# Interleaving the first attention step's transposed scores with the score groups of the second and third step

## The chip, the cores and the metric

One core of one Trainium2 chip. The metric is the device time of one launch in microseconds, the median of the runs; the kernel before took 898.83 us (three runs, 896.07 to 898.97).

## The reference

One layer of gated cross attention and a gated feed-forward part, in float32, for 8 sequences of 256 tokens, 512 wide; 32 query heads of 16 dimensions share 8 groups of keys and values. Cut to what matters here (the weights are plain matrices, `g_x` and `g_f` scalars):

```python
q = (layernorm(x) @ Wq.T)             # 32 heads of 16
k, v = ctx @ Wk.T, ctx @ Wv.T         # 8 groups of 16, each used by 4 heads
score = einsum('bhqd,bhkd->bhqk', q, k) / sqrt(16)
attn = softmax(score)
x = x + tanh(g_x) * ((attn @ v) @ Wfc.T + bfc)
h = layernorm(x)
x = x + tanh(g_f) * (shared_mlp(h) + routed_mlp(h) * sum_of_top2_weights)
```

## The kernel before

The tokens are worked through in 4 blocks of 512 (two sequences each); attention comes first for all blocks, then the feed-forward part. The attention of a block has 8 steps (`STEPS`), a step being one of two sequences and one of four chunks of 8 heads. Steps are counted through the launch: step 0 is the first of all, `n` its number.

A step has two passes over its scores. In the first, `sm_pair` (line 1325) computes scores with queries on partitions; a step has four such pairs, v = 0 to 3, and each pair is four matmuls of line 1336 that fill two PSUM banks. VectorE takes the maximum over keys from each bank (`maximum`, line 902), 8 of them a step, into `mcol`. TensorE transposes `mcol` (`mt_job`), ScalarE copies it negated to `mT` (`m_copy`, line 684), and SyncE puts it by DMA as one more row beside the queries (`put_max`, line 330, semaphore `m_rd`). In the second pass `st_pair` (line 1351) computes the transposed scores, keys on partitions, with the maximum already subtracted, into the two banks `STB` = bank 2 and 3; ScalarE exponentiates them into `probs` (line 757, 8 a step, two a pair). `pv_unit` (line 1361) multiplies with the values, and VectorE turns and divides the result (`o_turn` 1024, `inverse` 1028, `divide` 1034 and 1039).

`sm_bank` (line 210) says which bank a score group takes. Steps 0 and 1 use bank 0 to 3 in turn, so `st_pair` of step 0 must wait until the maxima of both are taken. All later steps take turns on banks 0, 1 and 5, beside the transposed scores in 2 and 3.

Each engine runs its own list in the order in which it is written. TensorE's: the maxima's scores of step 0, `mt_job(0, 0)`, the scores of step 1, then `body`, whose step s issues the scores of step s + 2 pair by pair with the transposed scores of step s. Between them stand the jobs that prepare the next block: `x_job` (line 1281) transposes a normalised tile `xn` into PSUM bank 6, where ScalarE (`x_high`, into `xnT_h`) and VectorE (`x_low`, line 877, into `xnT_l`) read it; the next `x_job` waits until `x_low` of the one before has run (semaphore `x_lo`). VectorE's list has the 8 maxima of step 0, the 8 of step 1, then `norm_rows(1)` (line 925), on which ScalarE's first normalised tile of the next block (`xn_tile(1, 0)`, line 621) waits, and then in `body` the maxima of step s + 2 with the other work of the step; there `x_low(1, 0)` stands behind the sixth maximum of step 2, and `x_low(1, 1)` behind the first of step 3. ScalarE's list has `xn_tile(1, 0)` behind the second exponential of step 0. GpSimd subtracts the context's high part (`cx_low`, line 442) beside them. None of the lists of VectorE, ScalarE, GpSimd and SyncE is touched.

Of the kernel before, what the change touches and what calls it, by code (L numbers as in the profile page):

```python
# [14 lines left out]
TILES = BLOCK // P  # L15
HC = P // DH
CHUNKS = HEADS // HC
# [3 lines left out]
UNITS = 8  # L21
# [22 lines left out]
def build(nc, x, ctxT, wq, wk, wv, wfc, bfc, g_x, g_f, w_gu, w_dn, w_r, out):  # L44
# [6 lines left out]
    with ExitStack() as ctx:  # L51
        def sem(name):
            return ctx.enter_context(nc.semaphore(name))
# [99 lines left out]
        bank = [ctx.enter_context(nc.psum_tensor(f"bank{i}", [P, 512], f32)) for i in range(8)]  # L153
# [17 lines left out]
        q_rd = [sem(f"q_rd{c}") for c in range(CHUNKS)]  # L171
        k_rd = [sem("k_rd0"), sem("k_rd1")]
        m_rd = sem("m_rd")
# [8 lines left out]
        xn_ok, x_tr, x_hi, x_lo, xb_ok = sem("xn_ok"), sem("x_tr"), sem("x_hi"), sem("x_lo"), sem("xb_ok")  # L182
        q_pr, q_hi, q_lo = sem("q_pr"), sem("q_hi"), sem("q_lo")
        k_pr, k_hi, k_lo = sem("k_pr"), sem("k_hi"), sem("k_lo")
        v_cp, vt_tr, vt_cp = sem("v_cp"), sem("vt_tr"), sem("vt_cp")
        f_mm, f_add, ln2_stats, ln2_var = sem("f_mm"), sem("f_add"), sem("ln2_stats"), sem("ln2_var")

        sm_full, st_full, max_ok = [sem("sm_full0"), sem("sm_full1")], [sem("st_full0"), sem("st_full1")], sem("max_ok")
        mt_tr, mt_cp = sem("mt_tr"), sem("mt_cp")
# [19 lines left out]

        def sm_bank(n, s, u):  # L210

            return bank[u % 4] if isinstance(n, int) and n < 2 else bank[(0, 1, 5)[(UNITS * s + u) % 3]]

        def x_bank(tb, j):

            return bank[j] if isinstance(tb, int) and tb == 0 else PJ[0]
# [656 lines left out]
        def _(dve):  # L873
# [22 lines left out]
            def maximum(n, s, u, par):  # L896
                qt, half, e = u // 4, u // 2 % 2, u % 2
                dve.wait_ge(sm_full[e], UNITS // 2 * n + u // 2 + 1)
                if u == 0 and not (isinstance(n, int) and n < 2):
                    dve.wait_ge(mt_tr, n - 1)  # L900
                at = mcol[:, par, e * HC + half * RH:e * HC + (half + 1) * RH].rearrange("p (j t) -> p j t", t=2)
                v.tensor_reduce(at[:, :, qt], sm_bank(n, s, u)[:, :].rearrange("p (r k) -> p r k", r=2),  # L902
                                AX.X, ALU.max).then_inc(max_ok, 1)
# [366 lines left out]
        def _(pe):  # L1270
# [9 lines left out]
            def tr(out, in_):  # L1280
                return nc.tensor.transpose(out, in_, ident[:, :])  # L1281

            def x_job(tb, j):
                pe.wait_ge(xn_ok, TILES * tb + j + 1)
                for c in range(DC):
                    last = tr(x_bank(tb, j)[:, c * P:(c + 1) * P], xn[:, j, c * P:(c + 1) * P])
                last.then_inc(x_tr, 1)
# [35 lines left out]
            def sm_pair(n, s, v, bb, c):  # L1323

                qt, half = v // 2, v % 2
                if isinstance(n, int) and n < 2:
                    if UNITS * n + 2 * v >= 4:
                        pe.wait_ge(max_ok, UNITS * n + 2 * v - 2)  # L1330
                else:
                    pe.wait_ge(max_ok, UNITS * n + 2 * v - (0 if s == 0 and v == 0 else 1))
                for j in range(2):
                    for e in range(2):
                        rows = slice(e * ROWS, e * ROWS + SM)
                        last = mm(sm_bank(n, s, 2 * v + e)[:, j * S:(j + 1) * S],  # L1336
                                  q_st[rows, c, 2 * half + j, qt * P:(qt + 1) * P], k_st[rows, bb, c, :],
                                  start=True, stop=True)
                        if j == 1:
                            last.then_inc(sm_full[e], 1)  # L1340

            def st_pair(n, v, bb, c):

                kt, half = v // 2, v % 2
                if isinstance(n, int) and n == 0 and v == 0:
                    pe.wait_ge(max_ok, 2 * UNITS)
                else:
                    pe.wait_ge(exp_ok, UNITS * n + 2 * v)
                for e in range(2):
                    rows = slice(e * ROWS, e * ROWS + ST)  # L1350
                    mm(STB[e][:, :], k_st[rows, bb, c, kt * P:(kt + 1) * P], q_st[rows, c, 2 * half:2 * half + 2, :],  # L1351
                       start=True, stop=True).then_inc(st_full[e], 1)

            def pv_unit(n, p, bb, c):

                kt, g2 = p // 2, p % 2
                pe.wait_ge(exp_ok, UNITS * n + 4 * kt + 4)
                if p == 0 and not (isinstance(n, int) and n == 0):
                    pe.wait_ge(ob_ok, n)
                for r in range(RH):  # L1360
                    last = mm(OTB[32 * r:32 * r + VW, g2 * S:(g2 + 1) * S], vals[:, bb, kt, 2 * c + g2, :],  # L1361
                              probs[:, p, r, :], start=p == 0, stop=kt == 1, skip_group_check=True)
                last.then_inc(pv_ok, 1)

            def mt_job(n, par):

                pe.wait_ge(max_ok, UNITS * n + UNITS)
                if not (isinstance(n, int) and n < 2):
                    pe.wait_ge(ob_ok, n - 1)
                tr(OTB[0:16, 0:P], mcol[:, par, :]).then_inc(mt_tr, 1)  # L1370
# [46 lines left out]
            for v in range(UNITS // 2):  # L1417
                sm_pair(0, 0, v, 0, 0)
            pe.wait_ge(q_lo, 3)
            mt_job(0, 0)  # L1420
            pe.wait_ge(q_rd[1], 64)
            for v in range(UNITS // 2):
                sm_pair(1, 1, v, 0, 1)
            pe.wait_ge(q_lo, CHUNKS)

            def body(t, first, last):
                nx = t + 1
                for s in range(STEPS):
                    n = STEPS * t + s
# [2 lines left out]
                    te = t if e < STEPS else nx  # L1432
                    be, ce = e % STEPS // CHUNKS, e % CHUNKS
                    look = not last or e < STEPS
                    for v in range(UNITS // 2):
                        if look:
                            if v == 0:
                                pe.wait_ge(q_rd[ce], 64 * (2 * te + be + 1))
                                pe.wait_ge(k_rd[be], 64 * (te + 1))
                            sm_pair(n + 2, e % STEPS, v, be, ce)  # L1440
                        if v == 0:
                            pe.wait_ge(m_rd, 32 * (n + 1))
                        st_pair(n, v, bb, c)
                        if v == 0 and not (first and s == 0):
                            for p in (2, 3):
# [77 lines left out]
                            continue  # L1523

                        if s == 0 and v == 1:
                            if first:
                                pe.wait_ge(k_lo, 1)
                            else:
                                pe.wait_ge(f_add, TILES * t - 2)
                            x_job(nx, 0)  # L1530
                        if s == 0 and v == 3:
                            pe.wait_ge(x_lo, TILES * nx + 1)
# [46 lines left out]
                        if s == 7 and v == 3:  # L1579
# [3 lines left out]
                            vt_job(nx, 0)  # L1583

            blocks(pe, body)

            for qt in range(2):
# [208 lines left out]
```

## Time and profile before

| | |
|---|---|
| median of the three runs | 898.83 us (896.07 to 898.97) |
| the profiled execution: its own time | 898.2 us |
| its span | 895.9 us |
| mean granted TensorE clock | 0.986 of full |
| TensorE matmuls busy | 864.9 us, 97% |
| VectorE busy | 636.0 us, 71% |
| ScalarE busy | 337.6 us, 38% |
| GpSimd busy | 480.7 us, 54% |

The span runs from the first to the last instruction; 2.3 us of the execution's own time lie around it. Starts are in us from the beginning of the span. A busy share is a mean over the launch: the stretch that the change touches begins near 38 us, where step 0's maxima are done, and it has to be read by itself.

### The profile page before, as it was taken

The page shows a single profiled execution, that of the slowest core. Times are in us where ns is not written, and L with a number is a line of the kernel's source. Part 1 is how long each engine was busy: PE and PEld are TensorE (multiplying, and loading weights), DVE is VectorE, ACT ScalarE, POOL GpSimd, SP SyncE. Part 2 cuts the span into 40 slices and gives each one's busy share as a digit, 9 for nine tenths or more (in the row PEclk, how much of TensorE's full clock was granted, in tenths as well). Part 3 has the DMA queues.
Part 4 walks back from the last instruction along what each step waited for, and adds up shares of the span by engine and source line. Part 5 has one row for each costly group of instructions (what it writes and reads, how often), then busy time and mean ns, then how long its engine had stood idle before and what let it go on. Part 6 is the DMA issues. An engine that isn't in the chain of part 4 may idle for free.

```text
span 895.9 us, 14888 instructions
## 1 busy us (share of the span) xinstructions
PE 864.9 (97%) x4923; PEld 643.1 (72%) x4923; DVE 636.0 (71%) x1085; ACT 337.6 (38%) x636; POOL 480.7 (54%) x485
## 2 busy tenths in 40 slices
PE   8699999999999899999999999998999999999998
PEld 6445665665565457888888888885788888888886
DVE  7789899889889956656565656667656565656565
ACT  4186586677657842212111211344211221122111
POOL 2314003002104999778667866754966786678640
PEclk9779999999999999999999999999999999999999
DMA  7753332432422113111211121112221112111102
GB/s 277 241 164 103 123 116 61 155 124 78 136 87 70 37 48 95 45 50 47 70 39 55 47 66 45 54 48 86 79 67 45 53 47 64 42 58 47 47 1 94
DMA packets 43609, 71.88 MB, mean 80 GB/s; under 512 B 6064, under 2 KB 21936, under 8 KB 43312
## 3 DMA queue, kind: packets, MB, share of 16 engines
q1 hardware_dynamic: 43568, 71.34, 24.6%
q8 instruction: 24, 0.39, 0.2%
q14 instruction: 17, 0.14, 0.0%
HBM read 55.33 MB, written 15.73 MB: 79 GB/s over the span
## 4 chain that ended last, share of the span: by engine, by line
PE 82%; DVE 11%; issue 3%; ACT 2%; DMA 1%; SPq 1%; POOL 0%; DVEq 0%; ACTq 0%; POOLq 0%
PE bank L1276 24%; PE bank L1277 23%; PE bank L1278 23%; DVE mcol L902 5%; PE bank L1336 4%; PE bank L1361 4%; PE bank L1351 3%; PE bank L1281 1%; DVE oN L1034 1%; PE bank L1670 1%; ACT probs L757 1%; DVE oB L1024 1%; DVE x_l L1241 1%; DMA q_scr<-qx_l 1%; DVE xnT_l L877 0%
## 5 line engine op out<-in xcount | busy, mean ns | idle before, releaser
L1276 PE MATMUL bank<-x_l,w_h 128*128 128x512 f32 x504 | 197.5, 392 | 2.5 <-DVE u L1112 2.5
L1278 PE MATMUL bank<-x_h,w_h 128*128 128x512 f32 x504 | 196.4, 390 | 0.0
L1277 PE MATMUL bank<-x_h,w_l 128*128 128x512 f32 x504 | 196.4, 390 | 0.0
L902 DVE TENSOR_REDUCE mcol<-bank 128x2 f32<-128x512 f32 x256 | 164.5, 670 | 25.2 <-PE bank L1336 24.5
L616 ACT ACTIVATE hT_h<-bank 128x512 fp32r<-128x512 f32 x72 | 43.1, 599 | 361.1 <-DVE bank L1214 352.2
L757 ACT ACTIVATE probs<-bank 128x512 f32<-128x512 f32 x256 | 139.0, 596 | 74.4 <-PE bank L1351 72.6
L572 POOL TENSOR_TENSOR w_l<-raw,w_h 128x512 fp32r<-128x512 f32 (+1 forms) x144 | 162.0, 1157 | 2.9
L1124 DVE SCALAR_TENSOR_TENSOR xa<-bank,tgf,xa 128x512 f32<-128x512 f32 x128 | 96.1, 751 | 77.7 <-PE bank L1278 77.6
L1276 PE MATMUL bank<-dn_l,hT_h 128*128 128x512 f32 x288 | 112.1, 389 | 1.7 <-issue 1.7
L1276 PEld LDWEIGHTS bank<-x_l,w_h 128*128 128x128 f32 x504 | 94.6, 188 | 25.9 <-DVE u L1112 3.9
L1278 PE MATMUL bank<-dn_h,hT_h 128*128 128x512 f32 x288 | 112.0, 389 | 0.0
L1277 PE MATMUL bank<-dn_h,hT_l 128*128 128x512 f32 x288 | 112.0, 389 | 0.0
L1278 PEld LDWEIGHTS bank<-x_h,w_h 128*128 128x128 f32 x504 | 94.7, 188 | 19.9
L1277 PEld LDWEIGHTS bank<-x_h,w_l 128*128 128x128 f32 x504 | 94.8, 188 | 19.1
L1112 DVE TENSOR_TENSOR u<-bank,r 128x512 f32<-128x512 f32 x72 | 49.7, 690 | 69.2 <-PE bank L1278 69.2
L442 POOL TENSOR_TENSOR cx_l<-cx_raw,cx_h 128x512 fp32r<-128x512 f32 x12 | 15.4, 1283 | 150.4 <-ACT cx_h L616 150.4
L581 POOL CAST dn_h<-dnraw 128x512 fp32r<-128x512 f32 x36 | 22.1, 613 | 111.6 <-PE bank L1278 93.8
L1336 PEld LDWEIGHTS bank<-k_st,q_st 48*128 48x128 f32 x512 | 40.2, 194 | 58.1 <-DVE mcol L902 38.4
L569 POOL CAST w_h<-raw 128x1792 fp32r<-128x1792 f32 x36 | 63.6, 1768 | 29.7 <-DVE x_l L1241 17.9
L1336 PE MATMUL bank<-k_st,q_st 48*128 48x256 f32 x512 | 66.7, 341 | 12.8 <-DVE mcol L902 11.6
L1361 PE MATMUL bank<-probs,vals 128*32 128x256 f32 x1024 | 70.1, 392 | 0.0
L1112 DVE TENSOR_TENSOR c<-bank,u 128x512 f32<-128x512 f32 x72 | 49.4, 686 | 24.0 <-PE bank L1278 23.9
(144 smaller groups left out, 1343.8 us busy)
## 6 DMA issues: line engine op xcount, KB each, us to landing
raw<-w_gu SPq DMA_DIRECT2D x36, 512.0 KB, 3.3
dnraw<-w_dn SPq DMA_DIRECT2D x36, 256.0 KB, 2.6
q_st<-q_scr SPq DMA_DIRECT2D x64, 128.0 KB, 2.6
q_scr<-qx_h SPq DMA_DIRECT2D x16, 256.0 KB, 2.1
q_scr<-qx_l SPq DMA_DIRECT2D x16, 256.0 KB, 2.3
q_st<-q_scr SPq DMA_DIRECT2D x64, 64.0 KB, 2.7
out<-xa SPq DMA_DIRECT2D x16, 256.0 KB, 2.0
cx_raw<-ctxT SPq DMA_DIRECT2D x14, 256.0 KB, 2.9
```

The costliest lines, as they stand in the source:

```text
L569: g.tensor_copy(w_h[f][:, :, :], raw[f][:, 0:7, :]).then_inc(gu_hi, 1)
L572: last = g.tensor_tensor(w_l[f][:, part, :], raw[f][:, part, :], w_h[f][:, part, :].bitcast(f32), ALU.subtract)
L616: return nc.scalar.activation(out, in_, ACT.Copy)
L757: nc.scalar.activation(probs[:, p, 2 * half:2 * half + 2, :], STB[e][:, :].rearrange("p (r q) -> p r q", r=2), ACT.Exp, scale=float(DH) ** ...
L902: v.tensor_reduce(at[:, :, qt], sm_bank(n, s, u)[:, :].rearrange("p (r k) -> p r k", r=2), AX.X, ALU.max).then_inc(max_ok, 1)
L1112: return v.tensor_tensor(out, psum[:, :], part[:, :], ALU.add)
L1124: v.scalar_tensor_tensor(tile, source[:, :], scale, tile, ALU.mult, ALU.add).then_inc(acc_ok, 1)
L1276: mm(out, a_h, b_l, start=start, stop=False, skip_group_check=onto)
L1277: mm(out, a_l, b_h, start=False, stop=False, skip_group_check=onto)
L1278: return mm(out, a_h, b_h, start=False, stop=stop, skip_group_check=onto)
L1336: last = mm(sm_bank(n, s, 2 * v + e)[:, j * S:(j + 1) * S], q_st[rows, c, 2 * half + j, qt * P:(qt + 1) * P], k_st[rows, bb, c, :], start= ...
L1361: last = mm(OTB[32 * r:32 * r + VW, g2 * S:(g2 + 1) * S], vals[:, bb, kt, 2 * c + g2, :], probs[:, p, r, :], start=p == 0, stop=kt == 1, s ...
```

## The change

`sm_bank` gives banks 0, 1 and 5 to step 1 as well; only step 0 keeps banks 0 to 3. The first transposed scores of step 0 then wait for the maxima of step 0 only. The body's step 0 of the first block is written out in `first_step`: the last two score pairs of step 1, and the first two of step 2, each stand ahead of a pair of step 0's transposed scores, and the last two pairs of step 2 follow behind them, with `x_job(1, 1)` between the two. `x_job(1, 0)` and `mt_job(1, 1)` change places. The wait for `q_lo` at 4 stands ahead of step 1's scores, as bank 5 was the last home of a query product.

```diff
         def sm_bank(n, s, u):
 
-            return bank[u % 4] if isinstance(n, int) and n < 2 else bank[(0, 1, 5)[(UNITS * s + u) % 3]]
+            return bank[u % 4] if isinstance(n, int) and n == 0 else bank[(0, 1, 5)[(UNITS * s + u) % 3]]
...
                 qt, half = v // 2, v % 2
-                if isinstance(n, int) and n < 2:
-                    if UNITS * n + 2 * v >= 4:
-                        pe.wait_ge(max_ok, UNITS * n + 2 * v - 2)
+                if isinstance(n, int) and n == 0:
+                    if v >= 2:
+                        pe.wait_ge(max_ok, 2 * v - 2)
                 else:
                     pe.wait_ge(max_ok, UNITS * n + 2 * v - (0 if s == 0 and v == 0 else 1))
...
                 if isinstance(n, int) and n == 0 and v == 0:
-                    pe.wait_ge(max_ok, 2 * UNITS)
+                    pe.wait_ge(max_ok, UNITS)
                 else:
                     pe.wait_ge(exp_ok, UNITS * n + 2 * v)
...
             pe.wait_ge(q_rd[1], 64)
-            for v in range(UNITS // 2):
+            pe.wait_ge(q_lo, CHUNKS)
+            for v in range(2):
                 sm_pair(1, 1, v, 0, 1)
-            pe.wait_ge(q_lo, CHUNKS)
+
+            def first_step():
+
+                for v in range(UNITS // 2):
+                    if v < 2:
+                        sm_pair(1, 1, v + 2, 0, 1)
+                    else:
+                        if v == 2:
+                            pe.wait_ge(q_rd[2], 64)
+                        sm_pair(2, 2, v - 2, 0, 2)
+                    if v == 0:
+                        pe.wait_ge(m_rd, 32)
+                    st_pair(0, v, 0, 0)
+                    if v == 1:
+                        pe.wait_ge(k_lo, 1)
+                        x_job(1, 0)
+                        pe.wait_ge(mt_cp, 1)
+                        mt_job(1, 1)
+                    if v == 2:
+                        pe.wait_ge(vt_cp, 1)
+                        pe.wait_ge(mt_cp, 2)
+                        for p in (0, 1):
+                            pv_unit(0, p, 0, 0)
+                sm_pair(2, 2, 2, 0, 2)
+                pe.wait_ge(x_lo, TILES + 1)
+                x_job(1, 1)
+                sm_pair(2, 2, 3, 0, 2)
...
                     look = not last or e < STEPS
+                    if first and s == 0:
+                        first_step()
+                        continue
                     for v in range(UNITS // 2):
```

TensorE's list before, from the transpose of step 0's maxima (`mcol`) on. `bank<-k_st,q_st` are score groups (four to a pair), `bank<-q_st,k_st` transposed scores (two to a pair), `probs,vals` the product with the values, `xn` an `x_job`.

```order
L1281 MATMUL bank<-ident,mcol 16x128
L1336 MATMUL bank<-k_st,q_st 128x256 x20
L1351 MATMUL bank<-q_st,k_st 128x512 x2
L1336 MATMUL bank<-k_st,q_st 128x256 x4
L1351 MATMUL bank<-q_st,k_st 128x512 x2
L1281 MATMUL bank<-ident,mcol 16x128
L1281 MATMUL bank<-ident,xn 128x128 x4
L1336 MATMUL bank<-k_st,q_st 128x256 x4
L1351 MATMUL bank<-q_st,k_st 128x512 x2
L1361 MATMUL bank<-probs,vals 32x256 x8
```

The four pairs of step 1 and the first of step 2 stand together as 20 matmuls, ahead of the first transposed scores.

The same place after the change, up to the second `x_job`:

```order
L1281 MATMUL bank<-ident,mcol 16x128
L1336 MATMUL bank<-k_st,q_st 128x256 x12
L1351 MATMUL bank<-q_st,k_st 128x512 x2
L1336 MATMUL bank<-k_st,q_st 128x256 x4
L1351 MATMUL bank<-q_st,k_st 128x512 x2
L1281 MATMUL bank<-ident,xn 128x128 x4
L1281 MATMUL bank<-ident,mcol 16x128
L1336 MATMUL bank<-k_st,q_st 128x256 x4
L1351 MATMUL bank<-q_st,k_st 128x512 x2
L1361 MATMUL bank<-probs,vals 32x256 x8
```

Only three pairs (12 matmuls) stand ahead of the first transposed scores; `x_job` now stands ahead of the transpose of `mcol`.

The end of step 0 and the start of step 1, as the difference of the two lists:

```order
-L1336 MATMUL bank<-k_st,q_st 128x256 x4
-L1351 MATMUL bank<-q_st,k_st 128x512 x2
+L1336 MATMUL bank<-k_st,q_st 128x256 x4
 L1281 MATMUL bank<-ident,xn 128x128 x4
-L1336 MATMUL bank<-k_st,q_st 128x256 x4
+L1336 MATMUL bank<-k_st,q_st 128x256 x8
```

Before, all pairs of step 2 stood ahead of the second `x_job`; now its last pair stands behind it, together with the first pair of step 3.

## Rows read from the trace of the kernel before

**Rows 1.** The page: busy time in us, share of the span and instructions of the engines
```profile
PE 864.9 (97%) x4923; PEld 643.1 (72%) x4923; DVE 636.0 (71%) x1085; ACT 337.6 (38%) x636; POOL 480.7 (54%) x485
```

**Rows 2.** Chain that ended last, 30 to 90 us: start, us, what
```profile
39.32 4.29 DVE mcol L902 x7
...
56.81 1.12 ACT probs L757 x2
...
62.74 0.69 DVE mcol L902
...
81.59 0.61 DVE mcol L902
82.20 0.04 issue
82.25 0.51 PE bank L1336 x4
```

**Rows 3.** VectorE in order of time: start, us, engine, operation, [idle before, releaser]
```profile
39.32 4.87 DVE L902 TENSOR_REDUCE mcol<-bank 128x2 f32<-128x512 f32 x8 [1.28 <-PE bank L1336]
44.12 0.15 DVE L925 SCALAR_TENSOR_TENSOR nmr<-mv,rstd 128x8 f32<-128x8 f32 x1
...
49.00 1.29 DVE L902 TENSOR_REDUCE mcol<-bank 128x2 f32<-128x512 f32 x2 [1.60 <-PE bank L1336]
50.21 0.68 DVE L877 TENSOR_TENSOR xnT_l<-bank,xnT_h 128x512 fp32r<-128x512 f32 x1
...
53.35 0.69 DVE L902 TENSOR_REDUCE mcol<-bank 128x2 f32<-128x512 f32 x1
```

**Rows 4.** TensorE in order of time, 38 to 53 us
```profile
41.86 0.80 PE L1336 MATMUL bank<-k_st,q_st 48*128 48x256 f32 x4 [0.40 <-DVE mcol L902]
43.74 0.79 PE L1336 MATMUL bank<-k_st,q_st 48*128 48x256 f32 x4 [1.09 <-DVE mcol L902]
44.34 0.80 PE L1351 MATMUL bank<-q_st,k_st 49*128 49x512 f32 x2
...
47.01 0.38 PE L1281 MATMUL bank<-ident,mcol 128*16 128x128 f32 x1
47.18 1.06 PE L1281 MATMUL bank<-ident,xn 128*128 128x128 f32 x4
48.17 0.80 PE L1336 MATMUL bank<-k_st,q_st 48*128 48x256 f32 x4
48.76 0.63 PE L1351 MATMUL bank<-q_st,k_st 49*128 49x512 f32 x2
49.33 1.93 PE L1361 MATMUL bank<-probs,vals 128*32 128x256 f32 x16
51.19 0.78 PE L1336 MATMUL bank<-k_st,q_st 48*128 48x256 f32 x4
...
52.13 0.66 PE L1281 MATMUL bank<-ident,xn 128*128 128x128 f32 x4
52.84 0.51 PE L1336 MATMUL bank<-k_st,q_st 48*128 48x256 f32 x4
```

**Rows 5.** ScalarE in order of time, 45 to 47 us
```profile
45.14 1.08 ACT L757 ACTIVATE probs<-bank 128x512 f32<-128x512 f32 x2 [6.19 <-PE bank L1351]
46.11 0.81 ACT L621 ACTIVATE xn<-xa,nmr,rstd 128x512 f32<-128x512 f32 x1
```

**Rows 6.** SyncE's issue of the maxima's row; landing times of the `q_st` transfers, 30 to 60 us
```profile
38.97 1.49 SPq L330 DMA_DIRECT2D q_st<-mT  x2
...
DMA to landing us min/median/max: 2.5/3.1/5.4
```

**Rows 7.** Stretches: PE, PEld, DVE, ACT, POOL busy (instructions), granted clock, DMA share, GB/s
```profile
34.00:35.00 1.00, 0.25 (x4) 0.04 (x2) 1.00 (x3) 0.00 (x0) 1.00 (x2) 0.87 0.66 206
40.00:41.00 1.00, 0.34 (x2) 0.34 (x4) 1.00 (x3) 0.00 (x0) 0.00 (x0) 0.50 0.02 4
51.00:52.00 1.00, 1.00 (x10) 0.70 (x6) 0.00 (x0) 0.00 (x0) 0.00 (x0) 0.59 0.90 270
57.00:58.00 1.00, 0.21 (x6) 0.03 (x2) 1.00 (x2) 1.00 (x4) 0.97 (x1) 1.00 0.51 134
59.00:60.00 1.00, 1.00 (x12) 0.21 (x4) 1.00 (x3) 1.00 (x3) 0.00 (x0) 0.50 0.02 4
62.00:82.00 20.00, 18.38 (x164) 10.55 (x162) 19.79 (x36) 14.84 (x30) 2.90 (x3) 1.00 0.23 69
```

**Rows 8.** GpSimd and VectorE near 57 us; all of L1034, ns min/median/max
```profile
57.03 1.27 POOL L442 TENSOR_TENSOR cx_l<-cx_raw,cx_h 128x512 fp32r<-128x512 f32 x1 [19.03 <-ACT cx_h L616]
57.05 1.52 DVE L1034 TENSOR_TENSOR oN<-oB,rden 128x256 f32<-128x256 f32 x1
...
L1034 DVE TENSOR_TENSOR oN<-oB,rden x31: 400/408/1540, 57.1 to 327.0; 128x256 f32<-128x256 f32 x31
```

More of the change, by code:

```diff
@@ L1525, in body @@
                         if s == 0 and v == 1:
[L1526 to L1529, printed above, removed]
+                            pe.wait_ge(f_add, TILES * t - 2)
                             x_job(nx, 0)
```

## The prediction

> **What bounds the kernel now.** I read the page first, then the chain of waits, then each engine in order of time. The page says that TensorE's matmuls are busy 97% of the span and VectorE 71% [rows 1], so on the whole TensorE is the bound. The chain of the stretch from 30 to 90 us says otherwise for that stretch: it runs over the maxima on VectorE, over ScalarE near 57 us, over VectorE again from 62.74 us, and only at 82.25 us does TensorE take over [rows 2]. From 62 to 82 us VectorE is busy 19.79 of 20 us while TensorE has 1.62 us without a matmul [rows 7]. VectorE's list has no slack there, so **whatever VectorE loses before 62.74 us, TensorE gets 82.25 us later by the same amount, and behind that point TensorE is the bound**. The question is therefore at what time VectorE, which does its work in an unchanged order, reaches fixed marks of its list. I use two: the first maximum of step 3, at 53.35 us [rows 3], and the maximum at 62.74 us [rows 2].
>
> From within the microsecond 34 to within the microsecond 51, and again around 60, TensorE runs at the lower of its two clocks, 1.2 GHz: 34 and 51 show the passages (0.87 and 0.59 as means), and 59 shows 0.50 [rows 7]. Durations for the change's place come from rows at that level.
>
> **Costs that I use.** At the low clock a score pair at 48.17 lets VectorE start at 49.00, 0.83 us later, and its successor on TensorE start after 0.59 us [rows 3, 4]. At the full clock the pair at 52.84 lets VectorE start at 53.35, 0.51 us later. A pair of maxima takes 1.29 us, of which the first is 0.69 [rows 3]. Transposed scores lead to an exponential 0.80 us later, two of which take 1.08 us [rows 4, 5]. The product with the values holds TensorE 1.86 us (49.33 to 51.19), `x_job` 0.99 us (47.18 to 48.17), the transpose of the maxima 0.17 us [rows 4]. TensorE answers a maximum in about 0.06 us, my estimate from the successions in these rows.
>
> **Part 1: step 1's scores on three banks.** Before, two pairs are computed ahead of need and the 8 maxima run without a gap, 39.32 to 44.12 us [rows 3]. With banks 5, 0, 1 the second pair's second half needs bank 5 back, so it starts only after the first maximum, at 40.07; VectorE can go on at 40.88, not 40.61. The third pair starts at 41.63 (maximum at 42.44). Then the first transposed scores follow at 42.23, and the fourth pair waits for the fifth maximum, 43.13: it starts at 43.19, and VectorE ends the eight at 45.29. That is three gaps of about 0.27 to 0.3 us and a pair that is itself answered late: **the maxima of step 1 end 1.17 us later** than 44.12. The moved wait for `q_lo` costs nothing: the split it guards stands behind the second maximum of step 0 in VectorE's list, well ahead of 39.32 us.
>
> **Part 2: the exponentials start earlier, but stop at once.** The first two start at 43.03 instead of 45.14 [rows 5], 2.1 us earlier, and end at 44.11. ScalarE's next item is the tile `xn`, which waits for `norm_rows(1)`, and that stands behind the eighth maximum: 45.42 instead of 44.27. So the tile runs 45.45 to 46.25 instead of from 46.11 [rows 5]: the 2.1 us have shrunk to 0.7.
>
> **Part 3: step 2's maxima come late.** Before, its first pair stood with step 1's scores at 43.74, and by 50.29 VectorE had taken six of the eight [rows 3, 4]. Now `x_job` (46.31) and the transpose of the maxima (47.3) stand ahead of the first pair: it starts at 47.5, and VectorE, idle since 45.8, takes two maxima from 48.3 to 49.6. Transposed scores (48.1) and the product with the values (48.7 to 50.5) come next, then the second pair at 50.5, and VectorE takes maxima from 51.35 to 52.65. At 52.65 it has taken four, where before it had taken six, and split a tile, by 50.9. The third pair needs bank space from the maximum that ends at 52.04; at 52.1, at the full clock, it gives maxima 52.65 to 53.9.
>
> **Part 4: the second `x_job` is now a barrier in front of the last pair.** It waits for `x_low(1, 0)`, which VectorE has behind the sixth maximum: 53.9 to 54.5 (0.68 us [rows 3]; before it ran at 50.21). `x_job` starts at 54.6 and the last pair 0.7 us behind it (52.13 to 52.84 [rows 4]), at 55.3: maxima 55.8 to 57.1. The first pair of step 3 waits for the seventh of them, 56.5, and VectorE starts step 3 at 57.05 if the clock is full. If it is low, `x_job` takes 0.99 and each pair 0.83, and it starts at 57.97. Against 53.35 this is **3.7 to 4.6 us later**. TensorE has a matmul in only about 1.6 of the 4.65 us from 51.7 to 56.35; before, the clock fell in a microsecond with 0.25 busy and behind one with 0.21 [rows 7], so I expect it to fall here, somewhere inside, and take 4.1.
>
> The moved DMAs: SyncE's list is the same, its waits for `mt_cp` come within 0.4 us of before, and the reads for step 4 move with the product they wait for, by about the same 3 to 4 us as their users.
>
> **Part 5: what step 1 gives back.** At 57.05 `divide` took 1.52 us, while its median over 31 is 0.408: 1.11 us more, beside GpSimd's subtraction from 57.03 to 58.30 [rows 8]. GpSimd follows ScalarE, which moves by less than VectorE, so that the two overlap for part of that time only: I give back 0.7 of a possible 1.1 us. The Trainium skill, SBUF — State Buffer, section on who interferes with whom, says that a VectorE operation with two SBUF inputs and a GpSimd operation that reads SBUF exclude each other for the whole instruction, so the later one waits until the other ends; by it the return is 0 if `divide` comes just behind GpSimd's start and all of it if it comes behind its end, and the trace agrees with it: `divide` ends 0.27 us behind GpSimd's end. The waits for low-clock matmuls in step 1 stay in either kernel; the bounds on their difference are 0.25 us less (none left) and nothing.
>
> **Sum:** 4.1 − 0.7 = **3.4 us**, between 3.7 − 1.35 = 2.35 and 4.6. The profiled execution took 898.2 us, so the forecast is **901.6 us**. The median of the runs is 0.6 us above that execution; a difference of 0.3%, about what a measurement of this kernel can tell from no change, is 2.7 us.
>
> **The rivals.**
> *The early exponentials win (not slower).* The chain passes over ScalarE near 57 us [rows 2], and if ScalarE set the pace up to there, an earlier start would count. For it: the last exponentials of step 0 start by my times at 51.9 instead of 52.24. Against it: VectorE has 19.79 of 20 us filled behind it, and has more left to do at 52 us. If VectorE's lag is taken up before 62.74, what stays is ScalarE's 0.3 us: 897.9 us; with the whole contention of `divide` gone too, 1.1 us more, 896.8. It decides if step 3's maxima start by 53.4.
> *The clock comes back one stage earlier.* TensorE works without a gap from 46.3 instead of 47.0 us. Full clock from 48 us on would halve the product with the values to 1.0 and shorten each answer by 0.3: step 3's maxima then start near 55.8, 2.4 late, less 0.4 given back: 900.2 us.
> *The clock doesn't come back at 51.4.* The third pair then takes 0.83, `x_job` 0.99: 1.3 us more than the mean case, 903 us with what is given back.
> *The first transposed scores don't come earlier at all.* They wait for `m_rd`. Its transfers are issued 38.97 to 40.46 us and need 2.5 to 5.4 us by the other `q_st` transfers [rows 6]: from the second issue, 39.7, that is 42.2 to 45.1. At 42.2 nothing is lost. At 45.1 the fourth pair, queued behind them on TensorE, would start at 45.7 instead of 43.19, and everything behind it 2.5 us later: 904.1 us. The DMA engines were busy 0.02 of the microsecond 40 [rows 7], so I take the short end. The Trainium skill, DMA: Bandwidth & Descriptors, in the anatomy of one DMA, has a fixed cost of about 2 us, most of it the receipt of the write; by it the row lies there at 41.7 or, from the end of the issue, 42.5, and this rival is nearly excluded.
>
> **How the numbers follow.** My forecast's case has 0.65: of its span, 2.35 to 4.6, three quarters lie over 2.7 us, so 0.49 slower and 0.16 no difference. ScalarE's rival 0.11: its own times are no difference, 0.06; the other 0.05 stand for more than it gives, under 895.5 us.  The early clock 0.10, same. The late clock 0.09 and the late row 0.05, both slower. Together: 0.05 faster, 0.32 same, 0.63 slower. The range of 8 in 10 reaches from 898.6, which takes in the early clock and leaves out most of ScalarE's rival, to 903.9, just short of the late row.
>
> **What would show each step right or wrong.** Right: the eighth maximum of step 1 ends near 45.3 us; the first exponential starts near 43.0 and the tile near 45.5; VectorE stands idle over 2 us ahead of step 2's first maximum at 48.3, and over 1 us ahead of its seventh, put down to TensorE's scores; step 3's first maximum starts at 57 to 58; TensorE takes over the chain at 85 to 87 us, and from there on the two traces run in parallel. Wrong: if step 3's maxima start near 53 us; or if they start at 57 and the end is still the same, because time is found between 62 and 82 us that the rows show as filled; or if the first transposed scores wait for a DMA until 45 us.

## The result, and the profile after

| | before | after |
|---|---|---|
| median (5 runs each) | 898.83 us | 901.86 us |
| lowest to highest | 896.07 to 899.24 | 901.17 to 903.22 |
| profiled execution: own time, span | 898.2, 895.9 us | 901.17, 899.3 us |
| mean granted clock | 0.986 | 0.987 |

The ratio of the runs is 1.0053, 95% interval 1.0038 to 1.0067: the change makes the kernel slower by 3.4 to 6.0 us, 4.8 as the middle. The medians alone lie 3.0 us apart, but three of the five runs before stand near 899 us and two near 896. The forecast was 901.6 us, from a loss of 3.4 us.

Maxima on VectorE in order of time, the changed kernel (start, us, engine, operation, [idle before, releaser]); they answer to [rows 3]:

```profile
39.41 1.29 DVE L902 TENSOR_REDUCE mcol<-bank 128x2 f32<-128x512 f32 x2 [1.28 <-PE bank L1336]
40.99 1.29 DVE L902 TENSOR_REDUCE mcol<-bank 128x2 f32<-128x512 f32 x2 [0.28 <-PE bank L1336]
...
44.13 1.29 DVE L902 TENSOR_REDUCE mcol<-bank 128x2 f32<-128x512 f32 x2 [0.28 <-PE bank L1336]
45.34 0.16 DVE L925 SCALAR_TENSOR_TENSOR nmr<-mv,rstd 128x8 f32<-128x8 f32 x1
...
48.61 1.29 DVE L902 TENSOR_REDUCE mcol<-bank 128x2 f32<-128x512 f32 x2 [2.75 <-PE bank L1336]
51.41 2.57 DVE L902 TENSOR_REDUCE mcol<-bank 128x2 f32<-128x512 f32 x4 [1.52 <-PE bank L1336]
53.90 0.68 DVE L877 TENSOR_TENSOR xnT_l<-bank,xnT_h 128x512 fp32r<-128x512 f32 x1
56.51 1.29 DVE L902 TENSOR_REDUCE mcol<-bank 128x2 f32<-128x512 f32 x2 [1.93 <-PE bank L1336]
58.15 0.69 DVE L902 TENSOR_REDUCE mcol<-bank 128x2 f32<-128x512 f32 x1 [0.35 <-PE bank L1336]
```

The forecast named all of these idle times, most of them nearly as long: 0.28 us three times among step 1's maxima, 2.75 ahead of step 2's first pair, 1.52 ahead of its second, 1.93 ahead of its last behind the second `x_job`. Step 3's first maximum starts at 58.15 us, 4.80 later than before.

ScalarE and TensorE there, the changed kernel; they answer to [rows 4, 5]:

```profile
42.99 1.08 ACT L757 ACTIVATE probs<-bank 128x512 f32<-128x512 f32 x2 [3.95 <-PE bank L1351]
45.59 0.81 ACT L621 ACTIVATE xn<-xa,nmr,rstd 128x512 f32<-128x512 f32 x1 [1.52 <-DVE nmr L925]
```

```profile
46.55 1.08 PE L1281 MATMUL bank<-ident,xn 128*128 128x128 f32 x4 [1.63 <-ACT xn L621]
47.42 0.42 PE L1281 MATMUL bank<-ident,mcol 128*16 128x128 f32 x1
47.78 0.80 PE L1336 MATMUL bank<-k_st,q_st 48*128 48x256 f32 x4
...
52.16 0.50 PE L1336 MATMUL bank<-k_st,q_st 48*128 48x256 f32 x4 [0.55 <-DVE mcol L902]
54.64 1.12 PE L1281 MATMUL bank<-ident,xn 128*128 128x128 f32 x4 [1.98 <-DVE xnT_l L877]
55.68 0.79 PE L1336 MATMUL bank<-k_st,q_st 48*128 48x256 f32 x4
```

The exponentials start 2.15 us earlier, ScalarE then waits 1.52 us for `norm_rows(1)`, and TensorE 1.63 us for the tile.

The chain that ended last, the changed kernel (start, us, what), where it passes to TensorE; it answers to [rows 2]:

```profile
86.11 0.61 DVE mcol L902
86.72 0.04 issue
86.76 0.50 PE bank L1336 x4
```

TensorE takes over at 86.76 us instead of 82.25, **4.51 us later, not 3.4**. The next 250 us run in parallel: the turn of the output (line 1024) is 4.51 us late in step 1 and 4.64 in the last step of attention, and VectorE's first accumulation of the feed-forward part (line 1124), at 365.25 us before, is 4.75 us late. The ends of the two spans differ by 3.4 us only, because of one place far behind the change. The stretch at the turn from the first to the second half of the tokens, before and then after (us busy of PE, PEld, DVE, ACT, POOL, then granted clock, DMA share, GB/s):

```profile
620.00:624.00 4.00, 2.97 (x10) 1.51 (x14) 2.31 (x5) 0.00 (x0) 3.92 (x3) 0.73 0.17 66
```

```profile
620.00:624.00 4.00, 3.92 (x18) 2.92 (x16) 4.00 (x9) 0.64 (x2) 1.96 (x1) 1.00 0.17 66
624.00:628.00 4.00, 2.21 (x14) 1.34 (x18) 2.89 (x6) 0.56 (x1) 3.92 (x3) 1.00 0.17 66
```

TensorE waits 1.86 us for VectorE (line 1112) there in both. Before, the clock fell to 0.5 behind that wait, for 3.4 us; in the profiled execution after it didn't, and the lag went from 4.76 to 3.41 us. That the profiled pair met the forecast's 3.4 us to a tenth is in part this accident; the runs' ratio says 4.8.

### The profile page after: what moved, and what is told of

It is laid out like the page before. It is cut to its first block, busy times and chain, and to the rows that moved or that the text cites. A ratio compares the mean times of both kernels' runs of the same rounds, so it can differ in the third digit from the quotient of the medians.

```text
span 899.3 us, 14887 instructions
## 1 busy us (share of the span) xinstructions
PE 863.6 (96%) x4923; PEld 642.1 (71%) x4923; DVE 636.0 (71%) x1085; ACT 338.3 (38%) x636; POOL 481.3 (54%) x485
## 4 chain that ended last, share of the span: by engine, by line
PE 81%; DVE 12%; issue 3%; ACT 1%; DMA 1%; SPq 1%; POOL 0%; DVEq 0%; ACTq 0%; POOLq 0%
PE bank L1276 24%; PE bank L1278 22%; PE bank L1277 22%; DVE mcol L902 5%; PE bank L1336 4%; PE bank L1361 4%; PE bank L1351 2%; PE bank L1281 1%; DVE oN L1034 1%; DVE oB L1024 1%; PE bank L1697 1%; DVE x_l L1241 1%; DVE xnT_l L877 1%; ACT probs L757 1%; DMA xa<-x 0%
```

## The experiments

Marks in the table are counted from the start of step 1's first maximum in each trace, since the stretch starts up to 1.4 us apart: S is the start of step 3's first maximum, T the turn of step 1's output (line 1024). The single executions of one kernel spread over 3 to 7 us, so parts are told apart by the marks, and what they are worth in all by the ratios. Each mark is read from one profiled execution. Where two profiles had the same order and the full clock up to S (the changed kernel with fill and with more fill, and likewise the moved pairs), S came out the same to 0.01 us. The ratios are to runs of the kernel before taken beside each kernel; its medians there were 897.15 us ("after, both" and the three with fill), 897.55 (the other four without fill), 898.00 (the three with more fill) and 897.35 (the last), so medians of different sets are not compared.

| kernel | S | T | median, us | ratio to before (95%) |
|---|---|---|---|---|
| before | 14.03 | 25.23 | | |
| after | 18.74 | 29.65 | 901.86 | 1.0053 (1.0038 to 1.0067) |
| banks only | 15.60 | 26.37 | 898.39 | 1.0008 (0.9995 to 1.0020) |
| after, `x_job` last | 17.62 | 28.50 | 901.20 | 1.0035 (1.0020 to 1.0050) |
| after, `norm_rows` early | 17.30 | 28.30 | 899.70 | 1.0030 (1.0014 to 1.0047) |
| after, both | 15.96 | 26.95 | 898.95 | 1.0022 (1.0008 to 1.0036) |
| before, pairs first | 13.29 | 25.38 | 897.57 | 0.9996 (0.9980 to 1.0013) |
| before, fill | 13.09 | 24.01 | 895.95 | 0.9984 (0.9973 to 0.9995) |
| after, fill | 14.92 | 25.11 | 896.60 | 0.9987 (0.9975 to 0.9999) |
| pairs first, fill | 11.58 | 23.35 | 896.44 | 0.9995 (0.9981 to 1.0009) |
| before, more fill | 12.15 | 23.82 | 895.68 | 0.9976 (0.9965 to 0.9987) |
| after, more fill | 14.92 | 25.11 | 897.35 | 1.0000 (0.9989 to 1.0012) |
| pairs first, more fill | 11.58 | 23.33 | 896.82 | 0.9991 (0.9977 to 1.0005) |
| the same, ten fills more in steps 0 to 2 | 12.93 | 24.79 | 895.46 | 0.9981 (0.9969 to 0.9993) |

**The parts of the loss.** First only the banks, on the kernel before, with the waits that belong to them (cut here to the line that chooses the bank):

```diff
-            return bank[u % 4] if isinstance(n, int) and n < 2 else bank[...]
+            return bank[u % 4] if isinstance(n, int) and n == 0 else bank[...]
```

> The kernel before, with only the banks of step 1's scores changed to 5, 0 and 1. Theory (the order of TensorE's list costs, each part by itself): the eighth maximum of step 1 ends at about 45.3 us instead of 44.12, step 3's first maximum starts about 1.0 us later than before (54.4 us), and the end is about 1 us later (899.5 us beside 898.5). Rival (the banks alone make most of the loss, since every pair is now answered late): step 3's first maximum starts 3 us or more later.

Step 1's maxima show the three gaps of 0.28 us, and S is 1.57 us late, T 1.14. The theory had about 1.0; the rival, 3 us or more, is out. In this execution the clock came back at 54.5 us and not at 51.8 as before, so a part of the 1.57 may be the clock's. The ratio's interval takes in no change.

Second, the barrier, on the changed kernel:

```diff
                 sm_pair(2, 2, 2, 0, 2)
+                sm_pair(2, 2, 3, 0, 2)
                 pe.wait_ge(x_lo, TILES + 1)
                 x_job(1, 1)
-                sm_pair(2, 2, 3, 0, 2)
```

> The changed kernel, with the second x_job behind the last score pair of step 2 instead of ahead of it. Theory (that x_job is a barrier: it waits for VectorE, and VectorE for the pair behind it): VectorE's idle 1.93 us ahead of step 2's seventh maximum goes, step 3's first maximum starts at 55.7 to 56.1 us instead of 58.15, and TensorE takes over the chain about 2.2 us earlier than in the changed kernel (84.6 instead of 86.76). Rival (the loss is made earlier, by step 2's first pair, and the x_job only sits in it; or the fall of the clock makes it): step 3's first maximum moves by under 0.8 us.

The idle 1.93 us went, as expected, but S moved by 1.12 us and T by 1.15: half of what the theory had. In this execution the clock stayed at the low level from 36.4 to 60.3 us, where the changed kernel had it full from 51.0 to 54.4, and the second and third pair of step 2 were answered at the low level:

```profile
51.85 1.29 DVE L902 TENSOR_REDUCE mcol<-bank 128x2 f32<-128x512 f32 x2 [1.73 <-PE bank L1336]
53.42 1.29 DVE L902 TENSOR_REDUCE mcol<-bank 128x2 f32<-128x512 f32 x2 [0.28 <-PE bank L1336]
```

Where the changed kernel has four maxima in a row from 51.41 us, here there is a gap of 0.28. TensorE's list is the same in both up to that place, so the order didn't keep the clock low there. That was the first sign that the clock, and not the order alone, decides how much of a wait is paid.

Third, the other gate: `norm_rows(1)` ahead of the loop over step 1's maxima.

> The changed kernel, with VectorE's norm_rows(1) ahead of step 1's maxima instead of behind them. Theory (ScalarE's tile waits for norm_rows and holds x_job and the first pair of step 2): the tile starts at about 44.1 instead of 45.59, step 2's first maximum at about 47.1 instead of 48.61, and step 3's first maximum 1.3 to 1.5 us earlier than in the changed kernel (56.7 to 56.9). Rival (the exponentials and the product with the values hold the rest of step 0 whatever the tile does): step 2's first maximum comes earlier, but step 3's by under 0.5 us.

ScalarE's tile no longer waits, step 2's maxima start 1.63 us earlier (counted from step 1's), and S is 1.44 us earlier. As the theory had it.

Fourth, both together:

> The changed kernel with both gates away: norm_rows(1) ahead of step 1's maxima, and the second x_job behind the last pair of step 2. Counted from the first maximum of step 1, the changed kernel is 4.4 us behind the kernel before at the turn of step 1's output, 3.3 without the x_job gate and 3.1 without the norm_rows gate. Theory (the gates add up, and the banks' 1.1 us and the late pairs stay): 1.8 to 2.2 us behind. Rival (the gates hide each other, one wait takes the other's place): over 2.7 us behind.

1.72 us behind at T, where the two singly take off 1.15 and 1.35 of 4.42, which leaves 1.92. The gates add up; what remains is a little more than the banks' 1.14.

**Is there something to win in the kernel before?** Its step 0 written out, with pairs moved ahead (only the bare order, several calls to a line; the waits are those of before):

```python
sm_pair(2, 2, 0, 0, 2); st_pair(0, 0, 0, 0)
sm_pair(2, 2, 1, 0, 2); st_pair(0, 1, 0, 0); mt_job(1, 1)
sm_pair(2, 2, 2, 0, 2); x_job(1, 0); st_pair(0, 2, 0, 0)
sm_pair(2, 2, 3, 0, 2); pv_unit(0, 0, 0, 0); pv_unit(0, 1, 0, 0)
st_pair(0, 3, 0, 0); sm_pair(3, 3, 0, 0, 3); x_job(1, 1)
```

> The kernel before, step 0 written out with score pairs moved forward: the third pair of step 2 ahead of x_job, the fourth ahead of the product with the values, step 3's first pair ahead of the second x_job. Theory (VectorE is the bound of 30 to 82 us, so what fills its idle time ends the stretch sooner): VectorE's idle 1.60 and 1.11 us near 48 and 51 us shrink, step 3's first maximum starts at 52.6 us or earlier instead of 53.35, and the end comes 0.7 to 1.5 us earlier than before. Rival (the slow clock makes TensorE's own work the bound there): step 3's first maximum stays within 0.3 us of 53.35 and so does the end.

S came 0.74 us earlier, as expected, and T 0.15 us later, so nothing was won: ratio 0.9996. In step 1 TensorE waits for ScalarE's exponentials, and VectorE for the pair behind the product with the values:

```profile
58.16 0.62 PE L1351 MATMUL bank<-q_st,k_st 49*128 49x512 f32 x2 [0.87 <-ACT probs L757]
58.71 1.94 PE L1361 MATMUL bank<-probs,vals 128*32 128x256 f32 x16
...
61.41 1.29 DVE L902 TENSOR_REDUCE mcol<-bank 128x2 f32<-128x512 f32 x2 [1.30 <-PE bank L1336]
```

The same place in the kernel before:

```profile
57.98 0.50 PE L1351 MATMUL bank<-q_st,k_st 49*128 49x512 f32 x2 [0.79 <-ACT probs L757]
58.41 1.76 PE L1361 MATMUL bank<-probs,vals 128*32 128x256 f32 x16
```

ScalarE, whose list is the same, starts the exponentials that TensorE waits for at 56.99 us here and at 56.81 before, and in both executions the clock falls behind that wait (0.69 in the microsecond 58 here, 0.82 before), and the product takes 1.94 and 1.76 us, where it takes 1.07 at the full clock. VectorE came to this place earlier, also because `divide` was over before GpSimd began (0.41 us instead of 1.52), and stood idle there: 2.23 us between S and T, 0.28 before. Moving the pairs moved VectorE alone, and ScalarE with the clock set the pace of step 1.

**How much of the loss is the clock?** Here the theory changed. What I had called the price of an order was the price at a low clock, and the order might be what lowers it. So the waits of TensorE were filled with matmuls on a spare bank whose results nobody reads:

```diff
+            pe.wait_ge(vt_cp, 1)
+
+            def fill(count):
+                for _ in range(count):
+                    mm(bank[7][:, :], k_st[:, 0, 0, 0:P], k_st[:, 0, 0:2, :], start=True, stop=True)
             for v in range(UNITS // 2):
                 sm_pair(0, 0, v, 0, 0)
+                fill((0, 3, 3, 6)[v])
...
             for v in range(UNITS // 2):
                 sm_pair(1, 1, v, 0, 1)
+                fill((0, 3, 3, 5)[v])
```

> The kernel before, with 26 matmuls on a spare bank (7) put into TensorE's waits between the score pairs of steps 0 and 1, so that its clock has no reason to fall; their results are not used. Theory (order and gates make 3.5 to 4 us of the loss in the changed kernel, the low clock the rest; before, the low clock costs too): the granted clock stays at full from 34 us on, pairs are answered in 0.51 instead of 0.83 us, step 3's first maximum starts at about 51 us instead of 53.35, and the end comes about 2 us earlier than before. Rival (the clock falls for another reason or these waits are bound by VectorE alone): clock still 0.5 from 35 us on, or step 3's first maximum within 0.5 us of 53.35.

(There are 23 of them, not 26.) The clock still fell at 34.5 us, came back at 38.0, and fell again from 48.2 to 51.6 and from 61.9 to 65.3. S is 0.94 us earlier, where 2.35 was expected, but the kernel is 0.16% faster by the ratio.

> The changed kernel, with such matmuls in its waits too, among them 5 behind the second transposed scores and 8 ahead of the second x_job. Theory (the order costs by itself): at full clock step 3's first maximum still starts 3.3 to 4 us behind that of the kernel before with fill, at about 54.8 us, and VectorE is idle over 1 us ahead of step 2's seventh maximum as well. Rival (the changed order costs because it lets the clock fall): the two kernels with fill lie within 1.5 us of each other at that mark.

S is 1.83 us behind the other kernel with fill, between theory and rival; the medians lie 0.65 us apart, and the two ratios tell no difference. But the two had not run at the same clock: this one kept it from 30 us on. Both were repeated with more fill (33 and 40 matmuls, with `wq_h` as operand, four ahead of step 0's first pair, which don't need the keys; the expectation below says 39 where there are 33):

> The kernel before, with fill matmuls in every wait from 31 us to the first transposed scores (39 of them, four ahead of step 0's first pair). In the first kernel with fill the clock still fell at 34 and at 48 us in the profiled execution; here it should stay at full to 62 us. Theory (the low clock costs the kernel before about 1.5 to 2 us): step 3's first maximum starts 1.5 to 2.0 us earlier than before, counted from the first maximum of step 1 (14.03 us behind it before, 12.0 to 12.5 here), and the end comes 1.5 to 2.5 us earlier than before. Rival (the fill itself delays as much as the clock gives): within 0.5 us of before.

> The changed kernel with as much fill. Two theories stand, after the changed kernel with fill was only 0.6 us slower than the kernel before with fill. If the order costs by itself and that result was flattered by the clock's fall in the other kernel: step 3's first maximum starts 2.3 to 3 us later than in the kernel before with more fill, the turn of step 1's output 1.5 us or more later, and the end 1.5 us or more later. If the low clock is nearly the whole of the loss: the turn of step 1's output and the end lie within 0.7 us of it.

Three stretches of the kernel before with more fill, then of the changed kernel with more fill (columns as above):

```profile
38.00:46.00 8.00, 7.02 (x42) 4.27 (x43) 7.55 (x15) 2.33 (x5) 0.00 (x0) 1.00 0.69 195
46.00:54.00 8.00, 7.28 (x71) 4.03 (x70) 6.71 (x13) 7.42 (x15) 0.00 (x0) 1.00 0.74 181
54.00:62.00 8.00, 6.83 (x54) 3.33 (x54) 7.55 (x12) 7.45 (x16) 2.75 (x2) 0.74 0.64 190
```

```profile
38.00:46.00 8.00, 7.15 (x38) 3.92 (x36) 6.30 (x13) 2.31 (x5) 0.80 (x1) 1.00 0.71 213
46.00:54.00 8.00, 6.77 (x53) 4.20 (x53) 5.25 (x9) 5.49 (x11) 0.00 (x0) 1.00 0.72 176
54.00:62.00 8.00, 6.75 (x67) 3.66 (x67) 7.91 (x15) 7.29 (x16) 1.81 (x2) 1.00 0.58 191
```

The granted clock is 1.00 in both up to 54 us, 2.4 GHz of the two levels, where the kernels without fill had 0.50 from 38 to 46. The mark S in the two, as the start of step 1's first maximum and the rows that hold step 3's first (the last of three in the second kernel, at 54.55 us), the kernel before and then the changed kernel:

```profile
38.42 4.88 DVE L902 TENSOR_REDUCE mcol<-bank 128x2 f32<-128x512 f32 x8 [0.88 <-PE bank L1336]
...
50.57 0.69 DVE L902 TENSOR_REDUCE mcol<-bank 128x2 f32<-128x512 f32 x1 [0.52 <-PE bank L1336]
```

```profile
39.64 5.24 DVE L902 TENSOR_REDUCE mcol<-bank 128x2 f32<-128x512 f32 x8 [0.88 <-PE bank L1336]
...
53.21 2.04 DVE L902 TENSOR_REDUCE mcol<-bank 128x2 f32<-128x512 f32 x3 [1.18 <-PE bank L1336]
```

That makes 12.15 and 14.92 us: **at the same clock, S is 2.77 us apart**. (VectorE's busy time in the 16 us shown, 14.26 and 11.55, differs by 2.7 as well, but 0.46 of that lies ahead of step 1's first maximum, since the second stretch begins later.) Without fill S is 4.71 us apart, **so 1.94 us of the loss up to S go with the low clock**, which makes the same order dearer. The fill itself holds back little: the second `x_job` starts 0.06 us behind `x_low` with and without it. It may have a part in the eight maxima of step 1, which take 5.24 us in the changed kernel and 4.88 in the kernel before.

At T the two are 1.29 us apart, and the theory had 1.5 or more. Two things cost the kernel before in this profile between S and T. The clock, expected full to 62 us, fell from 57.8 to 68.0, and the split of `aT` met GpSimd's subtraction (1.47 us against 0.69; `divide` lost 0.30 in the changed kernel). The changed kernel's profiled execution even ends 0.7 us earlier, with 1.4 us from the turn at 620 us, where the clock fell only in the other. So the end is read from the runs. The medians are 1.67 us apart, and the ratios, 0.9976 and 1.0000, say 2.1 us. Of the runs with a mean clock of 0.998 or more, the kernel before has seven, from 894.63 to 895.70 us, and the changed kernel ten, from 896.20 to 898.54: their medians are **1.75 us apart at nearly the same mean clock**. The first theory, an order that costs by itself, holds for 1.7 to 2.8 us, and the second, that the clock is nearly the whole, is out; neither alone makes 4.5. How the rest of the loss behind S divides between the clock and GpSimd was not tested.

Last, the moved pairs with fill:

> The kernel before with score pairs moved forward (as in the fourth run) and with fill in the waits of steps 0 and 1. Theory (VectorE's idle time is what can be won, and the low clock held the moved pairs back): step 3's first maximum starts by 50.7 us and the end comes 2.0 to 3.0 us earlier than before. Rival (ScalarE, which the moved x_job makes later, sets the pace of step 1): step 3 starts early, but TensorE takes over the chain no earlier than in the kernel before with fill alone.

> The kernel with score pairs moved forward and as much fill. Its first version with fill had runs from 893.9 to 900.2 us, by my theory because the clock fell in some of them. Theory: with more fill the runs draw together, the median is 894 to 895.5 us beside 897 to 898 for the kernel before, 1 to 1.5 us better than the kernel before with more fill. Rival (ScalarE's later start takes back what VectorE gains): no better than the kernel before with more fill.

S is 11.58 us, 2.45 less than before, of which 1.9 are left at T, and the profiled executions end 4.2 and 3.0 us earlier by their spans, 1.3 us of it at the turn at 620 us, where the clock fell only in the kernel before. But the runs don't confirm it: the ratios are 0.9995 and 0.9991, and neither tells a difference from the kernel before. They fell into two groups with more fill: six between 895.15 and 896.18 us at mean clocks of 0.996 to 1.000, four between 899.07 and 899.41 at 0.990 to 0.994, two between. The expectation that they would draw together was wrong, and so was that of a kernel 1 to 1.5 us better than the kernel before with more fill. Ten more fills followed, in steps 0, 1 and 2:

> The kernel with score pairs moved forward and fill, with ten more fill matmuls: two in the last wait of step 0, five in step 1, three in step 2, where TensorE waited 0.3 to 0.9 us for ScalarE or VectorE. Its runs without these fell into two groups, near 895.2 us at a mean clock of 1.000 to 0.998 and near 899.3 us at 0.990 to 0.994. Theory (in the second group the clock falls in steps 1 and 2, for want of work on TensorE): the second group goes, ten of twelve runs lie under 897 us, median 895.0 to 895.8. Rival (the clock falls elsewhere, or the fill delays what it precedes): the two groups stay, or the median is over 896.5 us.

The upper group has gone: ten of twelve runs lie under 897 us, the median is 895.46, both as expected. Four versions thus have an interval wholly below the kernel before: both kernels with the first fill (by 0.16 and 0.13%), the kernel before with more fill (0.24%), and this one (0.19%). Which of them is best the intervals don't tell. In this last profile the clock fell once between 46 and 54 us (mean 0.79), so the fills don't hold it in every execution.

## Why the prediction was right, and where it was off

**Part 1, the banks: right.** The eighth maximum ended at 45.42 us in the profile; forecast 45.29. The end before is 44.19 (39.32 + 4.87 [rows 3]) and not 44.12, which is the start of the next operation, so 1.10 us were forecast and 1.23 came. Alone, the banks cost 1.14 us at T.

**Part 2, the exponentials: right.** 42.99 against 43.03, the tile 45.59 against 45.45. The gate `norm_rows(1)` is worth 1.35 us at T, which the forecast carried in its times but did not price by itself.

**Part 3, step 2's first pairs: right.** 48.61 and 51.41 against 48.3 and 51.35.

**Part 4, the barrier: right in place, low in size.** The fall of the clock between the sixth and the seventh maximum came, in the microsecond 54 (0.70), and S is 4.80 us late, above the 4.6 of the low-clock case and well above the 4.1 taken as the mean. Taking a mean between a case with and one without the fall was the error, where [rows 7] spoke for the fall. This is the term that was mis-sized most: 4.1 forecast, 4.80 measured.

**Part 5, what step 1 gives back: wrong in the sum.** `divide` got back all 1.11 us, not 0.7: VectorE and GpSimd in the changed kernel

```profile
60.51 0.72 DVE L1024 STREAM_TRANSPOSE oB<-bank 128x512 f32<-128x512 f32 x1 [0.47 <-PE bank L1361]
...
61.20 1.28 POOL L442 TENSOR_TENSOR cx_l<-cx_raw,cx_h 128x512 fp32r<-128x512 f32 x1 [23.06 <-ACT cx_h L616]
...
62.51 0.41 DVE L1034 TENSOR_TENSOR oN<-oB,rden 128x256 f32<-128x256 f32 x1
...
65.78 1.27 POOL L442 TENSOR_TENSOR cx_l<-cx_raw,cx_h 128x512 fp32r<-128x512 f32 x1 [3.31 <-ACT cx_h L616]
66.29 1.04 DVE L877 TENSOR_TENSOR aT_l<-aT,aT_h 128x256 fp32r<-128x256 f32 x1
```

and the split of `aT` before:

```profile
62.13 0.47 DVE L877 TENSOR_TENSOR aT_l<-aT,aT_h 128x256 fp32r<-128x256 f32 x1
```

`divide` starts 0.03 us behind the end of GpSimd's subtraction, but the split of `aT` now meets the next one: 1.04 us instead of the 0.47 it took before, 0.57 lost again. It ends 0.28 us behind GpSimd's end (67.33 and 67.05), where `divide` ended 0.27 behind it before [rows 8]. This trace too agrees with the rule of the Trainium skill (SBUF — State Buffer, who interferes with whom), which the forecast did not apply to the other operation with two SBUF inputs. The low clock made VectorE wait another 0.47 us for the product with the values, and 0.25 us of VectorE's idle time in step 1 before are gone; together 0.22 us more, outside the forecast's bounds of nothing and 0.25 less. −1.11 + 0.57 + 0.47 − 0.25 = −0.32. So 0.3 us came back, not 0.7: 4.80 − 0.29 = 4.51 (0.29 by the marks, 0.32 by the rows).

**The sum.** 3.4 us was mis-sized: 4.5 us by the trace at the end of the stretch, within the stated span of 2.35 to 4.6 but at its end, and 4.8 by the ratio, just above it. Two terms erred the same way, 0.7 us in Part 4 and 0.4 in Part 5. That the median, 901.86, lies 0.3 us from the 901.6 forecast is in part luck: the forecast starts from 898.2 us, while the kernel before had medians of 897.15 to 898.00 in its four later sets of runs, and a base too high made up for a loss too small. In the chances, three quarters of the span of 2.35 to 4.6 were put over 2.7 us; spread evenly it would be 0.84.

**The statement that the traces run in parallel from there on** held for 530 us, to within 0.25 us, and failed at one place, the turn at 620 us, by 1.35 us of clock.

**The rivals.** ScalarE's early start gained nothing at S, 4.80 us late, and VectorE's lag was taken up nowhere between 62 and 82 us (VectorE is busy 19.90 of 20). The transposed scores did not wait for the maxima's row: they started at 42.32 us, right behind the pair ahead of them, so the row had landed within 3.3 us of the start of its first issue, 39.06. (The section of the Trainium skill that the prediction names for this, the anatomy of one DMA, describes a transfer issued on GpSimd's path; this row is issued by SyncE, so the trace decides and not the page's figure.) The clock came back at 51 us, as the main case had it.

## What to carry to other kernels

An engine whose average share is 71% can be the bound of the stretch that an edit touches; there the edit is priced by when that engine is next given work, pair by pair down the issuing engine's list, and one item in that list that waits for the bound engine (the second `x_job`) holds back all the work queued behind it. Look for a gate that stands behind what was moved, such as `norm_rows(1)`: exponentials started two microseconds earlier were worth nothing while it stood there, and moving it gave back 1.35 us. And where TensorE has long waits, price the order at both clock levels: the same order cost 4.71 us up to S with the clock low for most of it, and 2.77 with the clock full.

## What the runs showed of the hardware

The clock's fall is not the same from one execution to the next: in the profiles of these kernels it first fell between 34 and 37 us in eight, at 46.7 in one, at 57.8 in one and not at all in four before the last microseconds, and where it fell by 37 us it came back between 38 and 60 us. The kernel with moved pairs and more fill has runs of 895.15 us at a mean clock of 1.000 and 899.41 at 0.990. The clock and the time go together there, so a 0.3% difference between two single executions of such a kernel need not be an edit's; a mark in the trace that is counted from a common start tells parts apart much better. And unused matmuls in TensorE's waits were worth 0.24% (0.13 to 0.35) in the kernel before, though they do no work.
